# Graph convolution's corrections on 96 rows instead of five, and its bias added ahead

## What is computed

```python
def _gcn_conv(x, src, dst, W, b, n):
    h = x @ W
    deg = segment_sum(ones_like(dst), dst, n)
    dis = where(deg > 0, rsqrt(maximum(deg, 1.0)), 0.0)
    out = segment_sum(h[src] * (dis[src] * dis[dst])[:, None], dst, n)
    return out + b
...
h = relu(_gcn_conv(h, src, dst, W1, b1, n))
x = x + _gcn_conv(h, src, dst, W2, b2, n)
```

## Time and profile before

| what | value |
|---|---|
| median of 3 runs | 1907.78 us (1905.8 to 1908.43) |
| the profiled execution | 1907.54 us |
| its span, first to last instruction | 1905.7 us |
| mean granted TensorE clock | 0.993 |
| TensorE busy with matmuls | 1829.2 us (96%) |
| VectorE, ScalarE, GpSimd busy | 1383.8 (73%), 826.1 (43%), 455.0 (24%) |

### The profile page before, as it was taken

The page is one execution under the profiler, slowest core; times in us unless marked ns, Lnnn a source line. Parts: engine busy times, 40 slices in busy tenths (PEclk is TensorE's granted clock), DMA queues, the critical chain, the costliest instruction groups (busy, mean ns, idle before and its releaser), DMA issues. The chain is left out here.

```text
span 1905.7 us, 33972 instructions
## 1 busy us (share of the span) xinstructions
PE 1829.2 (96%) x11796; PEld 1572.4 (83%) x11796; DVE 1383.8 (73%) x2835; ACT 826.1 (43%) x1613; POOL 455.0 (24%) x544
## 2 busy tenths in 40 slices
PE   6898998999999999999999999999999999999998
PEld 3455887999889989998899899988998999887776
DVE  7697659888885498888854988888549888875323
ACT  1542455555542255554422554544225545446220
POOL 2000234111252241112512411125124111262000
PEclk9899999999999999999999999999999999999999
DMA  4112454110401121103011211030112110522001
GB/s 141 40 40 50 136 171 133 38 37 26 126 1 45 49 60 38 37 26 125 1 45 49 60 38 37 26 126 1 45 49 60 38 37 27 150 60 53 1 1 54
DMA packets 50752, 108.40 MB, mean 57 GB/s; under 512 B 18170, under 2 KB 18222, under 8 KB 50640
## 3 DMA queue, kind: packets, MB, share of 16 engines
q1 hardware_dynamic: 50608, 106.87, 19.2%
q0 software_dynamic: 32, 0.03, 0.0%
HBM read 83.62 MB, written 23.25 MB: 56 GB/s over the span
## 5 line engine op out<-in xcount | busy, mean ns | idle before, releaser
L869 ACT ACTIVATE PT<-ps 125x500 fp32r<-125x500 f32 (+1 forms) x480 | 214.3, 519 | 320.8 <-PE ps L1763 320.8
L1670 PE MATMUL ps<-PT,V 125*128 125x250 f32 x2400 | 313.3, 284 | 1.6 <-DVE PT L1274 1.6
L1670 PE MATMUL ps<-kT,qg 128*125 128x512 f32 (+1 forms) x1440 | 304.2, 356 | 8.2 <-DVE nmx L1258 6.9
L1670 PEld LDWEIGHTS ps<-kT,qg 128*125 128x125 f32 x1440 | 247.0, 187 | 59.6 <-issue 11.8
L1670 PEld LDWEIGHTS ps<-PT,V 125*128 125x128 f32 x2400 | 289.8, 190 | 2.9 <-DVE PT L1274 2.9
L1274 DVE TENSOR_TENSOR PT<-ps,PT 125x500 fp32r<-125x500 f32 (+1 forms) x480 | 253.0, 582 | 2.1 <-ACT PT L869 1.8
L1258 DVE CUSTOM_DVE_ANT_0 SB<-ps,bt 125x1250 f32<-125x1250 f32 x140 | 203.9, 1457 | 46.7 <-PE ps L1670 44.4
L1763 PE MATMUL ps<-ident,pbuf 125*125 125x125 f32 x1600 | 202.4, 274 | 12.7 <-DVE pbuf L1267 12.7
L1763 PEld LDWEIGHTS ps<-ident,pbuf 125*125 125x125 f32 x1600 | 187.2, 189 | 15.7 <-DVE pbuf L1267 15.0
L863 ACT ACTIVATE pbuf<-SB,nmx 125x1250 f32<-125x1250 f32 x140 | 188.1, 1344 | 12.6 <-DVE nmx L1258 11.1
L1267 DVE TENSOR_SCALAR pbuf<-pbuf,rden 125x1250 f32<-125x1250 f32 x160 | 151.2, 945 | 5.6
(11 more groups left out here) (243 smaller groups left out, 2819.0 us busy)
## 6 DMA issues: line engine op xcount, KB each, us to landing
bt<-edge_bias_scratch SPq DMA_DIRECT2D x40, 546.9 KB
q_scratch<-qc SPq DMA_DIRECT2D x16, 500.0 KB, 2.6
qc<-q_scratch SPq DMA_DIRECT2D x16, 500.0 KB, 4.8
counts_scratch<-cblk SPq DMA_DIRECT2D x10, 546.9 KB
c_rows<-counts_scratch SPq DMA_DIRECT2D x10, 546.9 KB
edge_bias_scratch<-b_rows SPq DMA_DIRECT2D x10, 546.9 KB
counts<-counts_scratch SPq DMA_DIRECT2D x10, 546.9 KB
wm<-in_L_gnn_wo_dram SPq DMA_DIRECT2D x4, 1024.0 KB, 8.7
```

What stands on the lines that cost most here:

```text
L869: sc.activation(PT[:, h % 2, 0, a:b, u * T:(u + 1) * T], ps_T[0:T, i, 0:(b - a) * T].rearrange("p (t n) -> p t n", n=T), ACT.Copy).then_in ...
L1670: e = mm(out_, lhs(a), rhs(b), start=start and i == 0, stop=stop and i == 2)
```

## The change

The operands of the rest matmuls, `rest5` and both `hs5`, get 96 rows (`DEEP`), of which VectorE writes the first five as before. GpSimd fills all 96 with zeros first: `hs5[0]` after its last self-loop addition, the other two after the last product of the stage `nodes`, whose operands lay there. VectorE waits for the three fills before it writes to the region. The bias `bvb` is added to z tile by tile in the stage of the product with W2, behind each `rows_low`; a finished tile then takes one operation, `z = ps * dis + z`, and TensorE waits for that one's semaphore.

```diff
+DEEP = 96
...
-        rest5 = place("rest5", [WIDE, N], F32R, r_qg)
-        hs5 = [place("hs5a", [WIDE, D], F32R, r_qc), place("hs5b", [WIDE, D], F32R, r_qg + 5024)]
+        rest5 = place("rest5", [DEEP, N], F32R, r_qg)
+        hs5 = [place("hs5a", [DEEP, D], F32R, r_qc), place("hs5b", [DEEP, D], F32R, r_qg + 5024)]
...
             for t in range(6, NT):
                 self_loop(t)
+            g.memset(hs5[0][:, :].bitcast(F32), 0.0).then_inc(s["g_z5"], 1)
+            pool.wait_ge(s["g_hs_mm"], NT)
+            g.memset(rest5[:, :].bitcast(F32), 0.0).then_inc(s["g_z5"], 1)
+            g.memset(hs5[1][:, :].bitcast(F32), 0.0).then_inc(s["g_z5"], 1)
             pool.wait_ge(s["g_wide"], 5)
...
             dve.wait_ge(s["g_b5"], 1)
+            dve.wait_ge(s["g_z5"], 3)
...
-            v.tensor_copy(hs5[0][:, :], ps[0:WIDE, 6, :]).then_inc(s["g_h5e"], 1)
+            v.tensor_copy(hs5[0][0:WIDE, :], ps[0:WIDE, 6, :]).then_inc(s["g_h5e"], 1)
...
-            v.tensor_tensor(rest5[:, :], wide_y[:, :], wide_hi[:, :].bitcast(F32), ALU.subtract).then_inc(s["g_b5"], 1)
+            v.tensor_tensor(rest5[0:WIDE, :], wide_y[:, :], wide_hi[:, :].bitcast(F32), ALU.subtract).then_inc(s["g_b5"], 1)
...
             for t in range(NT):
                 rows_low(NT + t, t % 2, t)
+                v.tensor_tensor(z[:, t, :], z[:, t, :], bvb[:, :], ALU.add).then_inc(s["g_fin"], 1)
             dve.wait_ge(s["g_h5"], 2)
-            v.tensor_copy(hs5[1][:, :], ps[0:WIDE, 2, :]).then_inc(s["g_h5e"], 1)
+            v.tensor_copy(hs5[1][0:WIDE, :], ps[0:WIDE, 2, :]).then_inc(s["g_h5e"], 1)
             for t in range(NT):
                 dve.wait_ge(s["g_ft"], t + 1)
-                v.scalar_tensor_tensor(out=ztmp[:, t % 2, :], in0=ps[0:T, t % 2, :], scalar=dis[:, t:t + 1], in1=bvb[:, :],
-                                       op0=ALU.mult, op1=ALU.add).then_inc(s["g_fin"], 1)
                 dve.wait_ge(s["g_fin"], t + 1)
-                v.tensor_tensor(z[:, t, :], z[:, t, :], ztmp[:, t % 2, :], ALU.add).then_inc(s["g_fz"], 1)
+                v.scalar_tensor_tensor(out=z[:, t, :], in0=ps[0:T, t % 2, :], scalar=dis[:, t:t + 1], in1=z[:, t, :],
+                                       op0=ALU.mult, op1=ALU.add).then_inc(s["g_fz"], 1)
...
             def last_rows(t):
 
                 if t >= 2:
-                    pe.wait_ge(s["g_fin"], t - 1)
+                    pe.wait_ge(s["g_fz"], t - 1)
```

More of the change, by code:

```diff
@@ L275, in build @@
                      "g_cnt g_c6 g_c7 g_c8 g_c9 g_x zx g_xd g_nb g_eye g_H g_dg g_diag g_bc g_disb g_hs_mm g_hh g_hs g_ag g_agd g_agr g_agh "
-                     "g_agT g_w2h g_w2 g_row g_tri g_wide g_gath g_h5 g_h5e g_b5 g_ft g_fin g_fz g_out z0 settled").split():
+                     "g_agT g_w2h g_w2 g_row g_tri g_wide g_gath g_h5 g_h5e g_b5 g_ft g_z5 g_fin g_fz g_out z0 settled").split():
             s[name] = sem(name)
```

## The result

The change takes the kernel from 1906.03 us (median of 8 runs, 1903.02 to 1908.43) to 1900.9 us (8 runs, 1898.98 to 1901.88): ratio 0.9968, 95% interval 0.9958 to 0.9979, which is 4.0 to 8.0 us. The forecast was 1901.1 us and 0.9965. The profiled execution took 1899.43 us (before 1907.54), its span 1897.7 (before 1905.7).

A forecast was written before the change was run, and what follows sets the result against it. TensorE was taken as the bound from 1788 us on. Savings of 5.9 (rows), 0.7 (bias) and 0 (fills) make 6.6 us, from 1907.54 to 1900.9; with 0.24 for the median, 1901.1 us, range 1899.2 to 1904.4.

The forecast's parts named there:

- The price of an excursion: Gathering stage and last product: going to a five-row matmul and back loses 0.36 to 0.38 us on TensorE.
- S1: Stretch from the first rest group to the last product's first matmul; forecast 55.5 us instead of 58.45.
- S2: Stretch from the last product's first matmul to VectorE's first operation on tile 9; forecast 4.88 instead of 5.25 us a tile.
- the sum: Whole change: 5.9 us from the rows, 0.7 from the bias, 0 from the fills, together 6.6 us saved.
- 96 rows for free: Rest matmuls: with 96 rows no stall is left, as for the 96-row condition rows; 5.9 us saved.
- The count: Eight full excursions in the gathering stage, seven in the last product, plus two ways in at 0.19 us each.
- The bias: End of the last product: one operation of 0.75 us replaces two, saving 0.7 us; ten moved additions priced 0.
- Rivals A and B: A: only the bias counts, 1907.1 us, chance 0.06. B: half of each excursion goes, 1904.4 us, chance 0.05.
- Rival C: GpSimd's fills end late and delay VectorE and the indirect load: 1911.6 us or more, chance 0.03.
- point of decision: Rival C's fills cost nothing until they end later than 1781.3 us; each microsecond beyond goes on the end.
- part 3: GpSimd's three zero fills: done by about 1762 us, 14 us before VectorE's wait, 4.8 more before rest5; price 0.

The follow-up runs named there:

- The rows alone: Kernel after with the bias part undone (96 rows and the fills kept, two operations a tile as before): 1900.02 us, ratio 0.9966 to before.
- The run with two excursions fewer: Kernel before, five rows throughout, with feature block 2's three rest matmuls in one group behind its three gatherings: 1905.06 us.
- 12 fills: Kernel after with the zero fill of rest5 done 12 times in a row, each waiting for the one before: 1896.93 us.

## Why the prediction was right, and where its working was not

**The price of an excursion.** It was worked out as 0.36 to 0.38 us from the steps between starts, not from the 0.42 of the chain's line. Both lines of the chain lose: the rest matmul's 0.18 and its followers' 0.19. The rows alone took 6.05 us off S1 and S2, against 5.9 in the sum.

**96 rows for free.** Carried over from another stage's 96-row matmuls, and borne out: S1 came to 55.47 us, against 55.5 at full steps throughout, and a tile of the last product takes 4.87 us (0.23 + 4.64), against 4.88.

**The count.** 15 full excursions and two ways in. At 0.37 and 0.19 us these come to 5.9, and 6.05 was measured. The run with two excursions fewer supports the unit.

**The bias.** 0.7 forecast, 0.70 measured. The ten additions cost nothing: S1, which holds their stage, is 58.44 with them and 58.45 without. That VectorE does 0.75 us of every 5.25 in the last product was read from one of its two operations; before the change it is 0.75 + 0.69. Nothing hangs on it, since both lie under TensorE's work.

**Rivals A and B** are refuted, by 64 against 65 rows and by S1 and S2 of the rows alone.

**Rival C** didn't happen, but its point of decision was wrong, and so was the fills' cover in part 3. The prediction put that point at 1781.3 us, by rest5. By the runs it is at the end of the copy, about 1777.2, so fills that end later than about 1775.6 cost; I had named a wait that is later in TensorE's order. The real fills end at 1760.6, 15 us ahead, so the forecast was not touched. Had they been some 16 us longer, the forecast would have missed a stall; a wait of 8.7 us would also have cost the clock, which the rival's "each microsecond on the end" leaves out. Nor is it so that the trace of before has no fill on GpSimd beside VectorE's work: the 96 x 1250 fill of the earlier trace rows runs beside small VectorE operations.

**The median.** That 1901.1 us was forecast and 1900.9 measured is closer than the working deserves, and partly luck. The forecast took its saving from a before of 1907.78 us (3 runs); over 8 runs before's median is 1906.03, and the same saving from there would give 1899.4. The medians differ by 5.1 us, 1.5 less than forecast, and the ratio's interval allows 4.0 to 8.0, so the runs' times bear out the size only roughly. It is the stretches, 6.75 against 6.6, that bear it out closely. The part ahead of them varies by more than that difference: the first rest group starts anywhere from 1785.0 to 1788.1 us in the nine profiled executions with no fills or the three of the change, and at 1784.3 with 12 fills. What makes that part vary wasn't studied.

## What to carry to other kernels

A matmul of few rows between full ones can cost more than its own length: look at whether its weight load, and the next one's, begin under the matmul before, and measure from start to start over the whole excursion. Where zeros can be filled in ahead of time, 65 or 96 rows made it disappear here; otherwise group such matmuls, since the price is by excursion. And before giving a new wait some cover, follow every wait behind it in the order of the engine that sets the time: the first is the one that counts.

## What the runs showed of the hardware

- A float32r contraction over 5, 32 or 64 rows between ones of 125 or 128 costs about 0.37 us there and back at a granted clock of 1.00, one over 65 or 96 nothing (S1 and S2 of the runs above).
- Weights of 5 columns for 125 rows (`sel`, L1899 before) have no such loss: on the chain of before, 10 matmuls of 512 columns from 1851.19 us on took 2.30 us, 0.23 each, and the 20 full ones behind them 4.62.
- Filling 96 x 1250 words with zeros on GpSimd took 1.14 us alone, and 21 in a row, each waiting for the last, 25.07 us, 1.19 each.
- TensorE's granted clock fell to 0.50 in a wait of 8.7 us and not in one of 2.7 us.
